# Graph attention: value units shared with GpSimd, loads from two queues, fillers on TensorE and new orders

## What is computed

```
h      = relu(layernorm(x))                       # 8192 x 256
z      = inlayer2 @ W.T + b                       # 8192 x 128
f1, f2 = z @ w1 + b1, z @ w2 + b2
coefs  = softmax(leaky_relu(f1[:, None] + f2[None, :], 0.01) - 1e9 * (1 - (adj > 0)))
out    = x + coefs @ h
```

## Time and profile before

| what | value |
|---|---|
| median of 3 runs | 1455.68 us (1455.66 to 1456.79) |
| the profiled execution | 1455.55 us |
| its span, first to last instruction | 1453.7 us |
| busy: PE, DVE, ACT, POOL | 97%, 88%, 42%, 18% of the span |
| granted TensorE clock, mean | 0.987 |
| HBM traffic | 208 GB/s over the span |

### The profile page before, as it was taken

How to read it: one execution, slowest core, us unless ns; L and a number is a source line. 1 busy time by engine, 2 the same in 40 slices (tenths; PEclk the granted TensorE clock), 3 DMA queues, 4 the chain that set the end, 5 groups by cost and what they waited for, 6 DMA issues and landing times.

```text
span 1453.7 us, 33309 instructions
## 1 busy us (share of the span) xinstructions
PE 1404.0 (97%) x12585; PEld 1241.2 (85%) x12585; DVE 1283.5 (88%) x1317; ACT 616.3 (42%) x726; POOL 256.6 (18%) x253
## 2 busy tenths in 40 slices
PE   7379999999999999999999999999999999999998
PEld 6257888888888888888888888888888888888887
DVE  5898999998998989898998989898998989898994
ACT  2777344434444434344443434344443434344430
POOL 0452111111111101111111111011111101111111
PEclk9789999999999999999999999999999999999999
DMA  9969999999999999999999999999999999999940
GB/s 294 280 142 200 228 230 230 229 229 229 218 214 211 210 209 215 208 212 209 215 209 209 215 209 210 207 217 210 209 215 209 211 208 216 206 211 212 213 104 8
DMA packets 110167, 302.41 MB, mean 208 GB/s; under 512 B 11716, under 2 KB 44612, under 8 KB 110148
## 3 DMA queue, kind: packets, MB, share of 16 engines
q1 hardware_dynamic: 100720, 291.68, 90.0%
q10 hardware_dynamic: 9428, 10.49, 2.6%
HBM read 293.73 MB, written 8.39 MB: 208 GB/s over the span
## 4 chain that ended last, share of the span: by engine, by line
PE 94%; DMA 3%; ACT 2%; DVE 1%; POOL 0%; issue 0%; SPq 0%; POOLq 0%; ACTq 0%; DVEq 0%
PE acc L990 61%; PE acc L992 30%; DMA adj_sb<-in_adj_dram 2%; PE rp L948 2%; DMA wgt<-in_L_gnn_inlayer_dram 1%; ACT mask L513 0%; ACT o_room L547 0%; ACT rp L513 0%; ACT h_f L534 0%; ACT H L540 0%; DVE wgt L789 0%; DVE wT L679 0%; SPq L315 0%; DVE c_word L775 0%; ACT o_room L534 0%
## 5 line engine op out<-in xcount | busy, mean ns | idle before, releaser
L990 PE MATMUL acc<-H,wT 128*128 128x257 f16 x8192 | 1357.7, 274 | 30.9 <-DVE wT L799 23.5
L992 PE MATMUL acc<-H,wT 128*128 128x257 f16 x4096 | 1120.8, 274 | 0.0
L990 PEld LDWEIGHTS acc<-H,wT 128*128 128x128 bf16 x8192 | 803.1, 98 | 133.9 <-DVE wT L799 24.0
L513 ACT ACTIVATE mask<-adj_sb 128x1024 bf16<-128x1024 int32 x504 | 519.3, 1053 | 545.1 <-DVE wgt L789 430.3
L799 DVE STREAM_TRANSPOSE wT<-wgt 128x1024 f32<-128x1024 f32 x512 | 633.3, 1238 | 129.6 <-PE acc L992 129.5
L789 DVE SCALAR_TENSOR_TENSOR wgt<-b_word,c_word,mask 128x1024 f32<-128x1024 f32 x504 | 627.6, 1257 | 4.0 <-ACT mask L513 3.9
L992 PEld LDWEIGHTS acc<-H,wT 128*128 128x128 f16 x4096 | 402.1, 98 | 50.4
L437 POOL TENSOR_TENSOR x_res<-o_room,x_res 128x256 f32<-128x256 f32 x64 | 68.5, 1070 | 1109.7 <-ACT o_room L520 1067.8
L520 ACT ACTIVATE o_room<-acc,r_den 128x256 f32<-128x256 f32 x64 | 30.2, 471 | 244.9 <-DVE r_den L818 244.8
L442 POOL TENSOR_TENSOR o_room<-o_room,x_res 128x256 f32<-128x256 f32 x64 | 80.7, 1261 | 5.3
L439 POOL TENSOR_SCALAR o_room<-h_mean,no_nb 128x256 f32<-128x256 f32 x64 | 61.9, 967 | 0.0
(11 more groups left out here) (88 smaller groups left out, 148.4 us busy)
## 6 DMA issues: line engine op xcount, KB each, us to landing
adj_sb<-in_adj_dram SPq DMA_DIRECT2D x508, 512.0 KB, 8.6
x_res<-in_x_dram SPq DMA_DIRECT2D x64, 128.0 KB, 4.1
out_dram<-o_room SPq DMA_DIRECT2D x64, 128.0 KB, 4.3
H<-in_x_dram ACTq DMA_DIRECT2D x16, 256.0 KB, 12.0
H<-in_x_dram SPq DMA_DIRECT2D x16, 256.0 KB, 13.2
...
```

The lines of the kernel that those rows point to most:

```text
L513: nc.scalar.activation(place, adj_sb[:, c, g * CQ:(g + 1) * CQ], ACT.Relu, scale=M_SCALE).then_inc(m_ready, 1)
L990: pe.matmul(acc[:, par, 0:DV], w_hi[:, slot, t, :], H[:, j, part, 0:DV], start=(j == 0 and part == 0), stop=False)
L992: mm = pe.matmul(acc[:, par, 0:DV], w_lo[:, slot, t, :], H[:, j, 0, 0:DV], start=False, stop=(j == ROWS - 1))
```

## The change

POOL makes units 3, 7, 11 and 15 of the values, as scale * x + bias without the relu (one `tensor_scalar` with two operations for each tile of 128 nodes); the relu of all units is taken in the high pass, now a Relu on ACT, and in the low pass of the odd units, which DVE makes. All roundings are on ACT, none on DVE. ACT issues quadrants 2 and 3 of row tile 1's adjacency, x6 and x7 stand earlier in its order, and so do the halves of row tile 0's second chunk. PE gets nine matmuls of ones ahead of the f products and ten ahead of the first product, and an order of its own for strips and sums. The chunks of the b exponents change places. Each strip of statistics has its own semaphore. The orders on POOL, ACT and DVE are new. `high_on_dve` is empty, and `two_rows` and `strip_order` stay as they were.

```diff
-stats_ready = sem("stats_ready")
+stats_ready = [sem(f"stats_ready{i}") for i in range(NS)]
...
+h_pool_ready = sem("h_pool_ready")
...
+high_on_dve = ()
+values_on_pool = (3, 7, 11, 15)
+def wait_values(eng, n):
+    before = sum(m < n for m in values_on_pool)
+    if n in values_on_pool:
+        eng.wait_ge(h_pool_ready, HALF * (before + 1))
+    else:
+        eng.wait_ge(h_ready, HALF * (n - before + 1))
+def wait_slot(eng, n):
+    if n == HR - 1:
+        eng.wait_ge(x_passes, 2 * TS * AS)
+    if n >= HR:
+        m = n - HR
+        wait_high(eng, m)
+        eng.wait_ge(lo_dve_ready if m % 2 else lo_ready, m // 2 + 1)
...
 def first_adj(eng, c, quadrants):
     eng.wait_ge(in2T_ready, 2 * (6 + 2 * c))
     load_adj(eng, 0, c, quadrants)
+def second_adj(eng, c, quadrants):
+    eng.wait_ge(m_ready, nth_part(0, Q - 1, c))
+    load_adj(eng, 1, c, quadrants)
...
         for n in range(NS):
             if n % Q == Q - 1 and not is_row(I, ROWS - 1):
                 sp.wait_ge(m_ready, nth_part(I, Q - 1, n // Q))
-                load_adj(sp, I + 1, n // Q)
+                load_adj(sp, I + 1, n // Q, (0, 1) if is_row(I, 0) else (0, 2, 1, 3))
...
     def D_column(k):
-        pool.wait_ge(h_ready, TS * (k + 1))
+        wait_values(pool, 2 * k)
+        wait_values(pool, 2 * k + 1)
         pool.wait_ge(D_parts_ready, 1)
         nc.gpsimd.tensor_copy(H[:, TS * k:TS * (k + 1), :, D],
                               D_parts[:, TS * k:TS * (k + 1), :]).then_inc(D_column_ready, 1)
+    def values(n):
+        pool.wait_ge(h_affine_ready, n // 2 + 1)
+        wait_slot(pool, n)
+        for t in range(HALF):
+            j = HALF * n + t
+            nc.gpsimd.tensor_scalar(h_slot(n)[:, t, :], x_stage(n // 2)[:, j % TS, :], h_mul[:, j:j + 1],
+                                    h_add[:, j:j + 1], ALU.mult, ALU.add).then_inc(h_pool_ready, 1)
     def low_of_values(n):
-        pool.wait_ge(h_ready, HALF * (n + 1))
+        wait_values(pool, n)
         wait_high(pool, n)
         nc.gpsimd.tensor_tensor(H[:, HALF * n:HALF * (n + 1), 1, 0:D], h_slot(n),
                                 H[:, HALF * n:HALF * (n + 1), 0, 0:D], ALU.subtract).then_inc(lo_ready, 1)
     rstds(0)
...
-    rstds(1)
     scale_D()
     affine(0)
+    rstds(1)
+    rstds(3)
     affine(1)
     parts_of_D()
     low_of_values(0)
+    values(3)
+    affine(2)
     D_column(0)
-    rstds(3)
-    affine(2)
+    affine(3)
+    low_of_values(2)
     rstds(4)
     D_column(1)
-    affine(3)
-    low_of_values(2)
+    low_of_values(4)
+    values(7)
+    D_column(2)
+    D_column(3)
     affine(4)
+    low_of_values(6)
     rstds(5)
-    D_column(2)
-    low_of_values(4)
+    rstds(6)
     affine(5)
-    low_of_values(6)
-    D_column(3)
-    rstds(6)
+    affine(6)
+    values(11)
+    low_of_values(8)
+    D_column(4)
+    low_of_values(10)
     rstds(7)
-    D_column(4)
-    low_of_values(8)
-    affine(6)
     D_column(5)
-    low_of_values(10)
     affine(7)
+    values(15)
     D_column(6)
     low_of_values(12)
     D_column(7)
...
+        act.wait_ge(b_ps_ready, c + 1)
...
+        wait_slot(act, n)
...
     def high_of_values(n):
-        act.wait_ge(h_ready, HALF * (n + 1))
-        nc.scalar.copy(H[:, HALF * n:HALF * (n + 1), 0, 0:D], h_slot(n)).then_inc(hi_act_ready, 1)
+        wait_values(act, n)
+        nc.scalar.activation(H[:, HALF * n:HALF * (n + 1), 0, 0:D], h_slot(n),
+                             ACT.Relu).then_inc(hi_act_ready, 1)
...
     sums(0)
     load_x(act, 1, 2, (2, 3))
+    f_to_sbuf(0)
+    load_x(act, 2, 3, (2, 3))
     squares(0)
-    load_x(act, 2, 3, (2, 3))
     load_x(act, 3, 4, (2, 3))
-    f_to_sbuf(0)
     first_adj(act, 0, (2, 3))
     load_x(act, 4, 5, (2, 3))
     sums(1)
     f_to_sbuf(1)
+    load_x(act, 5, 6, (2, 3))
     squares(1)
-    load_x(act, 5, 6, (2, 3))
+    load_x(act, 6, 7, (2, 3))
+    load_x(act, 7, 8, (2, 3))
...
+    b_of_chunk(0)
     b_of_chunk(1)
-    b_of_chunk(0)
     values(0)
     act.wait_ge(t_ps_ready, 1)
     nc.scalar.activation(c_f32[:, :].rearrange("p (c q m) -> p q c m", c=NCH, q=Q),
                          t_ps[:, 0:Q * ROWS].rearrange("p (q c m) -> p q c m", q=Q, c=NCH),
                          ACT.Exp).then_inc(c_exp, 1)
+    high_of_values(0)
     mask_part(0, 0, 0)
     mask_part(0, 1, 0)
-    load_x(act, 6, 7, (2, 3))
+    first_adj(act, 1, (2, 3))
     mask_part(0, 2, 0)
+    mask_part(0, 3, 0)
     values(1)
-    mask_part(0, 3, 0)
+    high_of_values(1)
     values(2)
-    values(3)
-    load_x(act, 7, 8, (2, 3))
-    high_of_values(1)
     high_of_values(2)
-    first_adj(act, 1, (2, 3))
+    second_adj(act, 0, (2, 3))
     values(4)
+    high_of_values(3)
+    high_of_values(4)
     values(5)
-    high_of_values(3)
     high_of_values(5)
+    mask_part(0, 0, 1)
     values(6)
-    mask_part(0, 0, 1)
+    high_of_values(6)
+    high_of_values(7)
     mask_part(0, 1, 1)
-    high_of_values(6)
-    values(7)
     mask_part(1, 0, 0)
-    high_of_values(7)
     mask_part(1, 1, 0)
     mask_part(1, 2, 0)
     mask_part(1, 3, 0)
     mask_part(0, 2, 1)
     mask_part(0, 3, 1)
+    second_adj(act, 1, (2, 3))
     values(8)
+    high_of_values(8)
     values(9)
     values(10)
     high_of_values(9)
-    values(11)
     high_of_values(10)
+    high_of_values(11)
     mask_part(1, 0, 1)
-    high_of_values(11)
     mask_part(1, 1, 1)
     mask_part(1, 2, 1)
     values(12)
+    high_of_values(12)
     mask_part(1, 3, 1)
     values(13)
+    mask_part(2, 0, 0)
+    mask_part(2, 1, 0)
+    values(14)
     high_of_values(13)
-    values(14)
-    values(15)
     high_of_values(14)
-    mask_part(2, 0, 0)
-    high_of_values(15)
-    mask_part(2, 1, 0)
     mask_part(2, 2, 0)
     mask_part(2, 3, 0)
+    high_of_values(15)
     scale_rows(0, 0, 0)
     def body(I, par, half):
...
+                               ).then_inc(stats_ready[j // TS], 1)
...
+        dve.wait_ge(stats_ready[k], TS // 2)
...
     chunk_f(0)
     raw_stats(16, 20)
+    chunk_f(1)
     raw_stats(20, 24)
-    chunk_f(1)
-    variance(2)
     dve.wait_ge(u_ready, Q + 1)
     then_wait(nc.vector.tensor_tensor(tiny[:, 4:5], cst[:, 0:1], cst[:, 1:2], ALU.add))
     dve.wait_ge(fm_ps_ready, 1)
     nc.vector.reduce_max(tiny[0:1, 1:2], fm_ps, AX.X).then_inc(f_max_ready, 1)
+    variance(2)
     raw_stats(24, 28)
     dve.wait_ge(F_ps_ready, 1)
...
-    def high_of_values(n):
-        dve.wait_ge(h_ready, HALF * (n + 1))
-        nc.vector.tensor_copy(H[:, HALF * n:HALF * (n + 1), 0, 0:D], h_slot(n)).then_inc(hi_ready, 1)
     def low_of_values(n):
         at = slice(HALF * n, HALF * (n + 1))
-        dve.wait_ge(h_ready, HALF * (n + 1))
+        wait_values(dve, n)
         wait_high(dve, n)
-        nc.vector.tensor_tensor(H[:, at, 1, 0:D], h_slot(n), H[:, at, 0, 0:D],
-                                ALU.subtract).then_inc(lo_dve_ready, 1)
+        nc.vector.scalar_tensor_tensor(out=H[:, at, 1, 0:D], in0=h_slot(n), scalar=0.0, in1=H[:, at, 0, 0:D],
...
+    then_wait(pack_b(0))
     then_wait(pack_b(1))
-    then_wait(pack_b(0))
-    high_of_values(0)
     dve.wait_ge(c_exp, 1)
     then_wait(pack(c_word[:, :], c_f32[:, :]))
     raw_stats(32, 36)
     raw_stats(36, 40)
     raw_stats(40, 44)
     weights(0, 1, 0)
+    weights(0, 2, 0)
     variance(4)
     raw_stats(44, 48)
-    weights(0, 2, 0)
     weights(0, 3, 0)
+    raw_stats(48, 52)
+    turn(0, 0)
     low_of_values(1)
-    turn(0, 0)
-    raw_stats(48, 52)
+    low_of_values(3)
     turn(0, 1)
+    raw_stats(56, 60)
+    raw_stats(52, 56)
     variance(5)
     turn(0, 2)
-    raw_stats(52, 56)
-    high_of_values(4)
-    low_of_values(3)
+    variance(6)
+    turn(0, 3)
     low_of_values(5)
-    turn(0, 3)
-    raw_stats(56, 60)
+    low_of_values(7)
     weights(0, 0, 1)
     weights(0, 1, 1)
-    raw_stats(60, 64)
     weights(1, 0, 0)
-    low_of_values(7)
-    variance(6)
     weights(1, 1, 0)
     weights(1, 2, 0)
     weights(1, 3, 0)
     turn(1, 0)
-    variance(7)
+    weights(0, 2, 1)
     turn(1, 1)
+    weights(0, 3, 1)
     turn(1, 2)
-    high_of_values(8)
-    weights(0, 2, 1)
-    weights(0, 3, 1)
+    raw_stats(60, 64)
     low_of_values(9)
     turn(0, 4)
+    variance(7)
     turn(1, 3)
+    low_of_values(11)
+    weights(1, 0, 1)
     turn(0, 5)
-    weights(1, 0, 1)
-    low_of_values(11)
     weights(1, 1, 1)
     weights(1, 2, 1)
     weights(1, 3, 1)
     turn(1, 4)
-    high_of_values(12)
     turn(1, 5)
     turn(0, 6)
     low_of_values(13)
     low_of_values(15)
     weights(2, 0, 0)
     weights(2, 1, 0)
-    weights(2, 2, 0)
-    weights(2, 3, 0)
     turn(1, 7)
     finish_0(0, 0, 0)
     finish_1(0, 0, 0)
     finish_2(0, 0, 0)
     dve.wait_ge(h_sum_done, 1)
     nc.vector.tensor_scalar(h_sum[:, :], hs_ps, 1.0 / (H_SCALE * N), None, ALU.mult).then_inc(h_sum_ready, 1)
+    weights(2, 2, 0)
+    weights(2, 3, 0)
...
+    pe.wait_ge(ones_ready, 1)
+    for n in range(9):
```

(38 more changed lines are left out.)

31 lines of the change are left out of this document (13 added, 18 removed).

## The result

The changed kernel took 1447.21, 1447.46 and 1449.13 us in its undisturbed runs (two more were disturbed and are left out), median 1447.46. The ratio to the kernel before is 0.995, with a 95% interval of 0.9937 to 0.9963: 5.4 to 9.2 us less than 1455.68. The profiled execution took 1447.21, 8.3 less than the 1455.55 of before; 4.6 less were forecast.

What follows compares the result with a forecast made beforehand. PE bounds the kernel, VectorE second, up to PE's landmark before row tile 2 at 138.44 us. Terms of -0.6 and -4.0 before the first product and 0.0 behind it took 1455.55 to 1451.0 us, range 1446 to 1458.

Steps and rivals of the forecast that it cites:

- (a): Before the packing of b: fillers, two more statistics, reordered b exponents and earlier x issues sum to -0.6 us.
- (b): Packing to first product: VectorE drops unit 0's rounding, waits less for GpSimd, makes two more statistics; sum -4.0 us.
- (c1): From turn(0,3): VectorE's nine instructions take 10.8 us, PE's work 6.6; PE waits 4.2 where 7.35 stood, -3.2 us.
- (c2): PE's 2.31 us wait in front of strip (1,4) hangs on the same four weights and a turn: 0.
- (c3): Ahead of row tile 2: two weights now behind the sum of values make PE wait, +2.3 us.
- (c4): First product to row tile 2: less waiting and fillers cut clock loss from 5.9 to about 3.6 us, -2.3.
- (c5): GpSimd's value units: 1.0 us per affine, 5 us per unit, so the lows behind them come late, +3.2 us.
- (a1): Before the first product: nine fillers give back time PE's f products lose at half rate, taken as -2.2 us.
- R4: Rival: loads fail, ACT stands at x7's issue with its queue full, half clock returns; 1454.9 us, chance 0.06.
- R3: Rival, fast side: GpSimd's units hidden (-3.2) and half of the third wait gone (-1.2); 1446.6 us, chance 0.13.
- R1: Rival, slower: GpSimd becomes the bound, units 7, 11 and 15 on the path; 1460 us at 1.84 per affine, chance 0.16.
- R2: Rival: beside GpSimd's affines, VectorE is held for each whole affine; 1454.0 us, chance 0.20.

Runs made afterwards that it cites:

- e2: The changed kernel without PE's nine and ten filler matmuls: 1449.0 us, 0.9955 of the kernel before.
- e3: The changed kernel with ACT's issues of x6 and x7 moved behind its two b exponentials: 1445.89 us, 0.9935 of the kernel before.
- e8: The changed kernel with ACT's loads (x6, x7, halves of chunk (0,1)) and row tile 1's adjacency as in the kernel before: 1459.02 us, 1.0027.
- e13: The kernel before with only the loads moved as in the change: 1451.02 us, 0.9968.
- e4: The changed kernel with weights(2,2,0) and (2,3,0) back ahead of the last transposition of row tile 1: 1446.61 us, 0.9938 of the kernel before.
- e12: The kernel before with only GpSimd's affines added for units 3, 7, 11 and 15: 1452.36 us, 0.9985.
- e5: The changed kernel with each GpSimd affine made as two instructions of one operation: 1462.1 us, 1.0045 of the kernel before.
- e6: The changed kernel with a second operation (an added 0.0) in GpSimd's product of h_mean, once per row tile: one run, 1448.31 us.
- e1: The changed kernel with GpSimd's value units 3, 7, 11 and 15 given back to ACT: 1454.17 us, 0.999 of the kernel before.

## Why the prediction was right, and where it was not

Forecast 1451.0, in a range of 1446 to 1458, and faster as the likeliest; measured 1447.2 in the profiled execution. The direction and half of the sum were right for their reasons, and the miss of 3.8 us is in the stretch behind the first product. Term by term, in us:

| step | forecast | measured | from |
|---|---|---|---|
| (a) to the packing of b | -0.6 | -0.4 | 52.64 to 52.24 |
| (b) packing to first product | -4.0 | -3.7 | 22.41 to 18.71 |
| (c1) waits of 1.79 + 5.56 | -3.2 | -3.1 | 4.28 |
| (c2) wait of 2.31 | 0 | -1.4 | 0.32 + 0.57 |
| (c3) weights behind the sum of values | +2.3 | +1.7 | 1.11 + 0.63 |
| (c4) clock | -2.3 | -1.8 | 63.39 - 9.66 = 53.73 to 58.83 - 6.91 = 51.92 |
| (c5) GpSimd's units late | +3.2 | 0 | no wait for GpSimd |

- (a) came out near by luck, by errors that cancel. (a1) was right (the copy 2.5 us earlier for 2.2, the nine fillers worth 1.8 to 1.9 of it in e2), and (a2) and (a3), forecast at 1.6 together, took 0.5: in e3, which has no stall, packing begins 8.0 us behind ACT's copy (42.89 to 50.93), 7.5 in before. But "the four x issues moved ahead of ACT's exponentials lie in its wait for f2" took them at 0.40 each, by a pair that had met no queue. The issues of x7 took 2.85 and 1.42, and put 1.6 more on that way (9.7 us, 42.57 to 52.24). R4 named this stall and gave it 1.6 (e3: 1.4 to 1.6), but tied it to loads that fail; the loads did what they say (e8, e13). It stood beside the forecast, not in place of it.
- (b) was right in its parts: c pack 0.45, no cast, the low of unit 1 at 1.19.
- (c1) was right in place, and in size by two misses that cancel: from turn(0,3) to turn(1,0) VectorE took 12.6 us (77.95 to 90.59) where 10.8 were counted, 1.9 of it in the low at 79.09, which stood for GpSimd's; PE was busy to 86.36, 8.4 us for 6.6.
- (c2) failed because only VectorE's own instructions were counted between the strips. The earlier trace rows has 3.9 us in which its weights stood for ACT's mask; the group of these weights now has 0.0. Part of the 2.31 was ACT's, and behind ACT's a load's: 2.17 of the 3.9 us are for a mask of row tile 1's second chunk, which SP alone had loaded and which ACT itself had waited for, a second wait for DMA beside the 5.46 that the forecast counted. In before:

```profile
109.56 1.06 ACT L513 ACTIVATE mask<-adj_sb 128x1024 bf16<-128x1024 int32 x1 [2.90 <-DMA adj_sb<-in_adj_dram]
```

- (c3) was right in place and near in size, and e4 shows that it was avoidable: VectorE stood 2.30 us for the sum of values, room for the two weights.
- (c4) was near in size, but not through the ten fillers, which gain nothing (e2). Nearly all of the 1.8 lies behind the third wait: there the clock had fallen behind 2.31 us of waiting (the window of before at e12: 0.91 over 19.41 us, 1.7 lost), and now, behind 0.57, it stays at 1.00:

```profile
110.06:129.78 19.72, 18.56 (x184) 15.26 (x185) 17.31 (x17) 11.29 (x14) 4.10 (x3) 1.00 0.79 172
```

  e12 shows the same with a wait of 1.54. So the gain went with the shorter third wait, (c2), which the forecast had at nothing, and not with less waiting in all: e12 waits 9.49 us for 9.66 and has it too.
- (c5) is the term that failed most. The price of an affine was taken from the nearest row, 0.92 us for one operation and one pointer, as 1.0. It took 0.54, because it has two operations (e5, e6). R3 ("GpSimd's units hidden", 1446.6, 0.13) is what happened. R1's time was near for what it assumed: with affines of 1.94 us the kernel took 1462.1, where R1 had 1460 for 1.84. In part that is luck, since R1 had only units 7, 11 and 15 on the path, and in e5 PE's first wait (3.94) is already for the D column behind unit 3.
- R2 falls for the affines: beside them VectorE's weights took 1.27 (62.25 us) and 3.77 for three (104.94), as elsewhere, and it is GpSimd that stands, 3.06 us in unit 15. VectorE does stand for GpSimd's lows, as it did before.
- What the prediction did not see is how its parts lean on one another. Alone in the kernel before, GpSimd's units give 3.0 us and the loads 4.4 (e12, e13); taken out of the changed kernel they cost 6.7 and 11.6 (e1, e8). The gap lies in the new orders: they ask for x7 and the masks so early that without the loads they are slower than before (e8). Whether the two parts together would give 7.4 us or more in the old orders, and what the new orders are worth by themselves, no run shows. The forecast valued ACT's relief at "waits for DMA go" and saw VectorE as the bound that is left. By e1 ACT is a second bound, 4.46 us late with all the affines. In before the loads hid this: ACT stood 5.46 us for a chunk anyway, and in e12, with less to do, 7.10.

The Trainium skill, page "GPSIMD Engine Reference", section 3.1, would have made 0.22 us (an estimate) of an affine over 256 columns. The runs show 0.54 with two operations and 0.93 with one: the rule pointed to the right side for two, at less than half of the measured time, and it knows no dearer single operation.
